# First attention: all queries projected in a stage over pairs of heads, kept in DRAM, and value products two key tiles behind the exponentials

## What is computed

```python
q = rmsnorm(x @ Wq_a) @ Wq_b            # 32 heads x 192
ckv = x @ Wkv_a                         # 64 compressed, 64 k_pe
kv = rmsnorm(compressed) @ Wkv_b        # per head: 128 k_nope, 128 v
q_pe, k_pe = rope(q_pe), rope(k_pe)
probs = softmax(causal([q_nope, q_pe] . [k_nope, k_pe] * 192 ** -0.5))
out = concat_heads(probs @ v) @ Wo
```

## Time and profile before

| | |
|---|---|
| median of 3 runs | 2994.73 us (2982.85 to 3002.94) |
| the profiled execution: time, span | 2989.91 us, 2987.7 us |
| TensorE busy | 2557.8 us (86% of the span) |
| VectorE, ScalarE, GpSimd busy | 1596.8, 1257.1, 633.4 us |
| mean granted TensorE clock | 0.912 |
| `mla_heads`, first instruction to last lift | 57.6 to 1021.7 us |

### The profile page before, as it was taken

How to read it: one execution, slowest core, us unless ns; L and a number is a source line. 1 busy time by engine, 2 the same in 40 slices (tenths; PEclk the granted TensorE clock), 3 DMA queues, 4 the chain that set the end, 5 groups by cost and what they waited for, 6 DMA issues and landing times. The chain is left out here.

```text
span 2987.7 us, 37616 instructions
## 1 busy us (share of the span) xinstructions
PE 2557.8 (86%) x12992; PEld 1325.8 (44%) x12992; DVE 1596.8 (53%) x2703; ACT 1257.1 (42%) x1756; POOL 633.4 (21%) x506
## 2 busy tenths in 40 slices
PE   4999999999999797739999995759999996999757
PEld 3566666666666573313332322323333323444434
DVE  3555555555556335457777746337787753011253
ACT  3444545444555422214565672214655663010331
POOL 1345444444545302310000002110000001001021
PEclk8899998989999998869999997879999998999778
DMA  2011111111011120120100000340111101100001
GB/s 63 17 34 34 38 37 27 37 34 37 27 43 31 66 72 21 61 69 1 28 14 15 14 1 15 91 99 1 38 28 23 22 1 57 71 0 0 16 0 53
DMA packets 72090, 99.79 MB, mean 33 GB/s; under 512 B 34392, under 2 KB 42840, under 8 KB 69680
## 3 DMA queue, kind: packets, MB, share of 16 engines
q1 hardware_dynamic: 71984, 98.27, 11.4%
HBM read 77.14 MB, written 20.84 MB: 33 GB/s over the span
## 5 line engine op out<-in xcount | busy, mean ns | idle before, releaser
L1937 POOL TENSOR_TENSOR l0a_p_low<-yT,l0a_p_high 128x1024 fp32r<-128x1024 f32 (+7 forms) x256 | 379.9, 1489 | 478.4 <-ACT l0a_p_high L1999 478.4
L1431 DVE TENSOR_REDUCE l2a_mx<-ps 128x1 f32<-128x512 f32 x512 | 338.1, 689 | 126.5 <-PE ps L1272 124.8
L1431 DVE TENSOR_REDUCE l1a_mx<-ps 128x1 f32<-128x512 f32 x512 | 337.0, 688 | 112.7 <-PE ps L1272 110.6
L1398 ACT ACTIVATE l2a_prob<-ps 128x1024 f32<-128x1024 f32 x256 | 250.7, 1019 | 131.7 <-PE ps L1311 93.8
L1398 ACT ACTIVATE l1a_prob<-ps 128x1024 f32<-128x1024 f32 x256 | 250.7, 1019 | 130.3 <-PE ps L1311 93.7
L1986 ACT ACTIVATE yT<-ps 128x1024 f32<-128x1024 f32 (+7 forms) x256 | 166.0, 648 | 276.2 <-PE ps L1869 174.8
L2052 DVE TENSOR_REDUCE l0a_mx<-ps 128x1 f32<-128x512 f32 (+3 forms) x384 | 203.9, 552 | 125.6 <-PE ps L1849 122.1
L1272 PE MATMUL ps<-l1a_k,l1a_q 96*128 96x512 bf16 x512 | 199.6, 399 | 65.0 <-DMA l1a_k<-l1a_k_parts 47.8
L173 POOL TENSOR_TENSOR applied<-prepared,neghalf 128x2 f32<-128x2 f32 x64 | 58.3, 911 | 900.3 <-DVE prepared L154 900.3
L1272 PE MATMUL ps<-l2a_k,l2a_q 96*128 96x512 bf16 x512 | 193.3, 391 | 46.4 <-DMA l2a_k<-l2a_k_parts 34.1
L1999 ACT CAST l0a_p_high<-yT 128x1024 fp32r<-128x1024 f32 (+7 forms) x256 | 172.0, 672 | 7.1
(11 more groups left out here) (291 smaller groups left out, 4570.0 us busy)
## 6 DMA issues: line engine op xcount, KB each, us to landing
l0a_woh<-in_l0a_wo SPq DMA_DIRECT2D x32, 256.0 KB, 2.6
l0a_cos_recip<-l0a_recip_row SPq DMA_DIRECT2D x32, 256.0 KB, 3.7
l0a_o<-l0a_o_pair SPq DMA_DIRECT2D x16, 512.0 KB, 2.7
yT<-l0a_o SPq DMA_DIRECT2D x16, 512.0 KB, 3.2
l0a_wqnT<-in_l0a_wqnT SPq DMA_DIRECT2D x32, 96.0 KB, 2.9
l1a_q_parts<-l1a_part SPq DMA_DIRECT2D x12, 256.0 KB
l1a_q<-l1a_q_parts SPq DMA_DIRECT2D x8, 384.0 KB
l2a_q_parts<-l2a_part SPq DMA_DIRECT2D x12, 256.0 KB
```

The costliest lines, as they stand in the source:

```text
L1398: nc.scalar.activation(prob[:, s % (2 * GROUP), :], ST[s % 2].rearrange("p b n -> p (b n)"), ACT.Exp, scale=SCALE).then_inc(s_exp, 1)
L1431: nc.vector.tensor_reduce(mx[:, m // NT, m % NT, c:c + 1], MB[c], AX.X, ALU.max).then_inc((s_red0, s_red1)[c], 1)
L1937: nc.gpsimd.tensor_tensor(p_low[:, j % 4, P * j:T], prob[:, j % 4, P * j:T], p_high[:, j % 4, P * j:T], ALU.subtract).then_inc(s_pl, 1)
```

## The change

A new block, `mla_queries`, stands between `latents` and `mla_heads`. It goes over 16 pairs of heads and does for a pair what jobs 0 to 3 did for a head: it projects the rotated part of both heads into one set of banks and the folded part of both into another, with five products of 128 rows per 512 columns (`project`: the 64-row parts are stacked, high above low, into `pe_rest` and `ab_rest`), rotates on VectorE, ScalarE and GpSimd, and stores the fp32 queries in a DRAM tensor `l0a_q`. The rotated query weights of all heads are loaded and split in `latents`. `mla_heads` loads one head's queries (`load`), rounds them in one piece at the end of a head (`cast`) and takes the rest on VectorE (`rest`). Its `PLAN` holds the 12 chunks alone, in steps 0 to 3, and the turn of the maxima follows in step 4. `pv` comes two tiles behind the exponentials, so the last two of a head fall into the next one, and the lift stands behind exponential 1 instead of exponential 0. Unchanged: chunks, scores, exponentials, value products and the third block.

```diff
+        q_dram = nc.dram_tensor("l0a_q", (MLA_HEADS, P, T), F32).ap()
...
+            act.wait_ge(s_pe_in, 32)
+            nc.scalar.copy(pe_high[:], pe0[:]).then_inc(s_pe_high, 1)
+            nc.scalar.copy(pe_rest[0:64, :], pe1[:]).then_inc(s_pe_high, 1)
...
+            dve.wait_ge(s_pe_high, 1)
+            nc.vector.tensor_tensor(pe_low[:], pe0[:], pe_high[:], ALU.subtract)
+            dve.wait_ge(s_pe_high, 2)
+            nc.vector.tensor_tensor(pe_rest[64:128, :], pe1[:], pe_rest[0:64, :], ALU.subtract)
...
+    cos, sin = sb("cos", [P, T]), sb("sin", [P, T])
+    n_high, n_low = sb("n_high", [P, 2, T], F32R), sb("n_low", [P, 2, T], F32R)
...
+    LAT, AB, VO = ps[:, 0:2, :], ps[:, 6, :], ps[:, 7, :]
+    def pe_banks(p):
+        return ps[:, 2 + 2 * (p % 2):4 + 2 * (p % 2), :]
...
+                ld(wqn[:, p % SLOTS], a["l0a_wqnT"][two].rearrange("h p r -> p h r"))
...
+            def store(p):
+                two = q_dram[2 * p:2 * p + 2]
+                sp.wait_ge(s_act, 6 * p + 8)
+                sp.dma_start(two[:, 0:KV_RANK, :], q_lat[:, p % 2, :]).then_inc(s_st[p % 2], 16)
+                sp.wait_ge(s_pool, 2 * p + 2)
+                sp.dma_start(two[:, KV_RANK:P, :], q_pe[:, p % 2, :]).then_inc(s_st[p % 2], 16)
...
+                    sp.wait_ge(s_pe, vo_at(p))
+                    load(p + SLOTS)
+            sp.wait_ge(s_st[0], 32 * (PAIRS // 2))
+            sp.wait_ge(s_st[1], 32 * (PAIRS // 2))
+            for i in range(2):
+                sp.dma_start(q32[:, i, :], q_dram[i]).then_inc(s_q[i], 16)
...
+                s = p % SLOTS
+                pe.wait_ge(s_ld[s], 64 * (p // SLOTS + 1))
+                for i in range(2):
+                    nc.tensor.matmul(AB[:, 64 * i:64 * i + 64], wqn[:, s, i, 0:P], wk[:, s, i, :], start=True, stop=True)
+                    mm = nc.tensor.matmul(AB[0:64, P + 64 * i:P + 64 * i + 64], wqn[:, s, i, P:Q_RANK], wk[:, s, i, :],
...
+            def project(banks, high, low, rest):
+                for c in range(2):
+                    cut = slice(512 * c, 512 * c + 512)
+                    nc.tensor.matmul(banks[:, c, :], high, n_high[:, 0, cut], start=True, stop=False)
+                    nc.tensor.matmul(banks[:, c, :], high, n_low[:, 0, cut], start=False, stop=False)
+                    nc.tensor.matmul(banks[:, c, :], low, n_high[:, 0, cut], start=False, stop=False)
+                    nc.tensor.matmul(banks[:, c, :], rest, n_high[:, 1, cut], start=False, stop=False)
+                    mm = nc.tensor.matmul(banks[:, c, :], rest, n_low[:, 1, cut], start=False, stop=True)
...
+            for p in range(PAIRS):
+                s = p % SLOTS
+                if p >= 2:
+                    pe.wait_ge(s_act, 6 * p - 5)
+                    pe.wait_ge(s_dve, 5 * p - 2)
+                project(pe_banks(p), pe_high[:, pair], pe_low[:, pair], pe_rest[:, pair]).then_inc(s_pe, 1)
+                pe.wait_ge(s_act, high_at(p))
+                pe.wait_ge(s_dve, 5 * p + 5)
+                project(LAT, ab_high[:], ab_low[:], ab_rest[:]).then_inc(s_pe, 1)
+                if p + 1 < PAIRS:
+                    absorb(p + 1)
+                if p:
+                    pe.wait_ge(s_act, 6 * p + 5)
+                for i in range(2):
+                    mm = nc.tensor.matmul(VO[64 * i:64 * i + 64, :], wv[:, s, i, :], woh[:, s, i, :],
+                                          start=True, stop=True)
+                mm.then_inc(s_pe, 1)
...
+                act.wait_ge(s_pe, absorbed_at(p))
+                nc.scalar.copy(ab_high[:], AB[:, 0:P]).then_inc(s_act, 1)
+                nc.scalar.copy(ab_rest[0:64, :], AB[0:64, P:2 * P]).then_inc(s_act, 1)
...
+            for p in range(PAIRS):
+                act.wait_ge(s_pe, 4 * p + 2)
+                if p >= 2:
+                    act.wait_ge(s_pool, 2 * p - 2)
+                for i in range(2):
+                    nc.scalar.copy(turned[32 * i:32 * i + 32, p % 2, :], raw[32 - 32 * i:64 - 32 * i, :]).then_inc(s_act, 1)
+                act.wait_ge(s_pe, 4 * p + 3)
+                    act.wait_ge(s_st[p % 2], 32 * (p // 2))
+                nc.scalar.copy(q_lat[:, p % 2, :], wide(LAT)).then_inc(s_act, 1)
+                if p + 1 < PAIRS:
+                    absorbed(p + 1)
+                act.wait_ge(s_pe, vo_at(p))
+                nc.scalar.copy(wo[:, p, :], VO).then_inc(s_act, 1)
...
+                pool.wait_ge(s_act, 6 * p + 7)
+                nc.gpsimd.tensor_tensor(turned[0:64, b, :], turned[0:64, b, :], sin[0:64, :], ALU.mult).then_inc(s_pool, 1)
+                pool.wait_ge(s_pool, 2 * p + 1)
+                pool.wait_ge(s_dve, 5 * p + 8)
+                nc.gpsimd.tensor_tensor(q_pe[:, b, :], straight[:, b, :], turned[:, b, :], ALU.add).then_inc(s_pool, 1)
...
+                dve.wait_ge(s_pe, 4 * p + 2)
+                for i in range(2):
+                    nc.vector.tensor_tensor(turned[64 + 32 * i:96 + 32 * i, b, :], raw[96 - 32 * i:128 - 32 * i, :],
+                                            sin[64 + 32 * i:96 + 32 * i, :], ALU.mult).then_inc(s_dve, 1)
+                dve.wait_ge(s_act, 6 * p + 7)
+                nc.vector.tensor_tensor(straight[:, b, :], raw, cos[:], ALU.mult).then_inc(s_dve, 1)
+                if p + 1 < PAIRS:
+                    absorbed(p + 1)
...
             def load(n, par):
-                def ld(dst, src):
...
-                sp.wait_ge(s_womm, n - 1)
-                load(n, par)
+                sp.wait_ge(s_low, n - 1)
+                sp.dma_start(q32[:, par, :], q_dram[bass.ds(n, 1)].rearrange("h p t -> p (h t)")).then_inc(s_q[par], 16)
...
             with sp.Fori(0, NH // 2 - 3) as i:
+                load(i * 2 + 5, 1)
                 spread(i * 2 + 1)
-                reload(i * 2 + 5, 1)
...
+            PLAN = [(0, 1, 2, 3), (3, 4, 5, 6), (6, 7, 8, 9), (9, 11, 12, 12)] + [(NMAX,) * 4] * 4
...
-                    if j == 0 and not last:
-                        job(h + 1, 1 - par, next_turn, 0, False)
-                    if j == 0 and not first:
-                        pv(h - 1, NT - 1)
+                    chunks(j, 0)
+                    if j < 2 and not first:
                     pe.wait_ge(s_exp, h * NT + j + 1)
                     if j + 2 < NT:
                         scores(h, par, j + 2)
                     elif not last:
                         scores(h + 1, 1 - par, j + 2 - NT)
-                    if not last:
-                        for k in range(*PLAN[j][0:2]):
-                            job(h + 1, 1 - par, next_turn, k, False)
-                    if j == 1 and not first:
+                    chunks(j, 1)
+                    if j == TURN_STEP and not last:
+                        max_turn(h + 1, 1 - par)
+                    if j == 2 and not first:
                         pe.wait_ge(s_os, h)
-                    if j:
-                        pv(h, j - 1)
-                    if not last:
-                        for k in range(*PLAN[j][1:3]):
-                            job(h + 1, 1 - par, next_turn, k, False)
+                    if j >= 2:
+                        pv(h, j - 2)
+                    chunks(j, 2)
...
-                nc.gpsimd.tensor_tensor(q_low[:, par, cut], q32[:, cut], q_high[:, par, cut],
-                                        ALU.subtract).then_inc(s_low, 1)
...
+            def cast(par, turn):
+                act.wait_ge(s_q[par], turn * 16 + 16)
+                nc.scalar.copy(q_high[:, par, :], q32[:, par, :]).then_inc(s_high, 1)
...
-                    if j == 0 and not last:
-                        ready(h + 1, 1 - par, next_pair, 0)
-                    if j == 0 and not first:
+                    if j == 1 and not first:
                         if not second:
...
-                    if j and not last:
-                        ready(h + 1, 1 - par, next_pair, j)
+                if next_turn is not None:
+                    cast(par, next_turn)
...
+            def rest(n, par):
+                dve.wait_ge(s_high, n + 1)
+                nc.vector.tensor_tensor(q_low[:, par, :], q32[:, par, :], q_high[:, par, :],
+                                        ALU.subtract).then_inc(s_low, 1)
```

More of the change, by code:

```diff
@@ L1466 @@
 RMS_EPS = 1e-6
-JOBS = 17
 MAX_CHUNKS = []
@@ new lines, in max_chunk @@
+                elif n == 1:
+                    if not first:
+                        pe.wait_ge(s_mrow, h)
+                else:
+                    pe.wait_ge(s_red, h * NMAX + n - 1)
+                mm = nc.tensor.matmul(b[:, 0:width], q_high[:, par, qt * P:(qt + 1) * P],
+                                      k_high[:, 512 * c:512 * c + width],
+                                      start=True, stop=dg is None)
+                if dg is not None:
+                    mm = nc.tensor.matmul(b[:, dg:dg + P], unit[:], mask[:], start=False, stop=True)
@@ L1879, in pv, with head, chunks @@
                 mm.then_inc(s_pv, 1)
```

(38 more changed lines are left out.)

340 lines of the change are left out of this document (173 added, 167 removed).

## The result

| | before | after |
|---|---|---|
| median | 2998.84 us (4 runs) | 3088.40 us (4 runs, 3083.65 to 3094.16) |
| ratio, 95% interval | | 1.030 (1.024 to 1.036) |
| span of the profiled execution | 2987.7 us | 3092.4 us |
| TensorE busy, mean granted clock | 86%, 0.912 | 78%, 0.891 |
| first chunk | 83.09 us | 435.31 us |

The change made the kernel 3% slower; the forecast was 4% faster. The last three rows divide the miss (first chunk and lifts as in the earlier trace rows). The heads took about what was forecast, and a pair of heads in the new block took nearly three times the time planned for it (22.2 us, not 7.95).

A forecast was written before the change was run, and what follows sets the result against it. TensorE's own instructions were taken to bound the heads. New block +124, heads -238, first chunk to first lift -6 and last head -3 gave -123 us: 2867 us for the profiled execution, forecast median 2872 us, range 2830 to 2935.

The forecast's parts named there:

- The heads: Attention heads without the projection: 21.3 us each instead of 29.23, over 30 heads -238 us.
- the part on the new block: Query block ahead of the heads: TensorE-bound, 7.95 us per pair, first chunk at 207.3 us instead of 83.09, +124 us.
- the ends: First chunk to first lift 39.9 us instead of 46.0, -6 us; last head 11.9 instead of 14.7, -3 us.
- what follows the last lift: Third block, behind the heads: forecast not to move.
- the sum for the block's end: New block's end: copies, GpSimd, store, read back, roundings and split take 17.6 us, TensorE covers 4.4, so 13.2 us idle.
- The rule that was weighed in the prediction: New block's 128-row products: no weight load hidden, 0.42 us each, sum -63 us; the prediction followed the trace's 0.233 instead.
- the first rival: New block's products as slow as the old projection's, 0.42 us each: +60 us, 2932 us; chance 0.10.
- The wait for exponential 2: In each head, ScalarE's lift and rounding delay exponential 2 to 6.2 us; TensorE asks at 5.4, waiting 0.8 us.
- lower bound of 20.3 us: Heads with no wait showing: 20.3 us each; as a rival -30 us, 2842 us, chance 0.12.
- The distance of two: Value products two tiles behind exponentials in the heads: costs nothing; a distance of one would lose about 0.8 us a head.
- the rival at half clock: New block stays at half clock since fp32 folds interrupt it: 14.5 us a pair, +105 us, 2977 us; chance 0.04.
- the forecast case: Whole kernel at 2872 us, own range 2838 to 2915 (heads 20.5 to 22.3, pair 7.5 to 8.6, start 0 to +20); chance 0.62.

The follow-up runs named there:

- e1_all16: Changed kernel with both stores of a pair's queries cut into one DMA per head; 2848.0 us, 0.953 of the time before.
- e8_lag2_b: e1_all16 with queries of heads 0 and 1 read back early, chunks re-placed, turn of the maxima behind step 4's value product; 2832.0 us, 0.947 of before.
- e9_lift2: e8_lag2_b with ScalarE's lift of the last head's sums behind exponential 2 instead of exponential 1; 2801.4 us, 0.937 of before.
- e4_lag1: e1_all16 with value products one key tile behind the exponentials and the lift behind exponential 0 again; 2829.6 us, 0.947 of before.

## Why the prediction was wrong, point by point

- **The step that failed** is in the part on the new block: "DMA moves 1.9 MB per pair; 172 GB/s took 0.48 of the engines, so 358 GB/s is full and 1.9 MB take 5.4 us. All less than TensorE". It spread the stores over all DMA engines. They ran on two, at 53 GB/s, and took 19.8 us a pair. The pair was sized at 7.95 us and took 22.2; the first chunk came at 435.3 and not 207.3 us. That is +228 us; the heads came out 11 us shorter than forecast, the ends 3 us longer and what follows the last lift 8 us longer, together +227 or +228 us. The profiled execution misses its 2867 us by 227; the medians miss by 216, since this execution lies 6 us above its median and the one before lay 5 us under. Also the sum for the block's end took 2.7 us for a store "as the store of the same size"; that store, `l0a_o<-l0a_o_pair`, has 128 rows as its slowest dimension. Same bytes, another form. No rival covered it either: all of them were about TensorE and ScalarE.
- **With that one step mended the number held**: e1_all16 took 2848.0 us, within 1% of 2872 and inside the range. For the heads that is in part luck (below). What is left of the miss is small and of known place. The pair took 6.7 to 7.1 us, not 7.95, mostly since the two value folds take 1.1 us and not 2.0 (the one of each head writes its own half of the partitions; their four rows start at 168.96, 169.11, 169.44 and 169.54 us, and the next projection at 170.07). First chunk 16.7 us early; heads 30 * 0.36 = 11 us less; first chunk to first lift 41.6 and not 39.9 us.
- **The products of `project`** stand 0.23 us apart at full clock, as forecast:

```profile
220.63 0.40 PE L1799 MATMUL ps<-l0q_n_high,l0q_ab_high 128*128 128x512 f32 x1
220.86 0.39 PE L1800 MATMUL ps<-l0q_n_low,l0q_ab_high 128*128 128x512 f32 x1
221.09 0.39 PE L1801 MATMUL ps<-l0q_n_high,l0q_ab_low 128*128 128x512 f32 x1
```

  The rule that was weighed in the prediction (the Trainium skill, "TensorE: Matmul & The Clock Gate", Part 3: weight loads overlap only across row groups) would have given 0.42; the trace disagrees, and the first rival falls.
- **The heads**: 20.92 us, forecast 21.3; the clock was 1.00 from the first lift to the last. The size was right and the reason wrong. The wait for exponential 2 was computed rightly, 0.8 us against 0.75 measured in e8_lag2_b, but in the changed kernel the waits for reductions, 1.4 us a head, come ahead of it and swallow it. The prediction had it the other way round ("most of that wait falls into the same 0.8 us"). Its 20.5 us of products were too many as well: e9_lift2's whole head takes 19.56 us with 0.23 us of listed wait left, so they are 19.3 us at most, and its lower bound of 20.3 us was none. Too much for products and too little for waits cancelled: that is the luck.
- **The distance of two**: costed at nothing, with 0.8 us a head to be lost at one. Undoing it gained 0.51 us a head (e4_lag1). The prediction looked only at what value product 0 waits for, not at what it covers for VectorE where it stands. With chunks and lift placed for it the distance of two is no loss (e9_lift2); its 0.8 us a head against a distance of one was never tested with all else the same.
- **The block's end**: 13.2 us of TensorE's wait forecast, 14.7 measured in e1_all16. **What follows the last lift**, forecast not to move, took 2987.7 - 1020.7 = 1967.0 us before, 3092.4 - 1117.3 = 1975.1 us after, and 1964.6 to 1971.6 us in the other nine traces, with the same instructions. The granted clock there was 0.90 in the changed kernel and 0.91 before and in e1_all16; no experiment looked at these 8 us. The pair's DMA time with all engines in use wasn't 5.4 us of 7.95 (0.68): the window has 0.90 and 277 GB/s, 308 GB/s when full. DMA was near to being the next bound.
- **Two slips in its sums**, without effect on the forecast: a pair with 4.66, 1.04 and 2.0 us doubled takes 15.65 and not 14.5 us, so the rival at half clock is 2995 and not 2977 us; and the three highs of the forecast case together give 2929 and not 2915 us.

## What to carry to other kernels

Cost a DMA by its form, not by its bytes: write down the slowest dimension of both sides, and if it is 2, expect two engines' worth of bandwidth, and every other transfer that shares those two engines to queue behind it. In a profile the sign is a low DMA share (here 0.13, or 0.24 with other traffic) while everything waits for DMA and SyncE's issues take microseconds. When work is moved within a hand-written order, ask of each moved piece both what it waits for and whose wait it was covering, and re-place what was put there for the old distance (here the lift: 30 us).
